# Three changes of order in a fused attention stage on one core: the residual addition ahead of the statistics, the input's transpose between two blocks of transposes, and a subtraction in halves

## The reference, cut to what matters

```python
x = x + L0_xattn(layernorm(x), ctx, ctx)      # 128 sequences of 64 rows, width 128, 16 heads of 8, causal
x = x + L0_ffn(layernorm(x))                  # 64 experts, top 8 of 64, plus one shared expert
x = x + L1_xattn(layernorm(x), ctx, ctx)      # correlation by FFT, top 6 delays
x = x + L1_ffn(layernorm(x))                  # quantised input, ternary weights

# L0_xattn: one matrix Wq projects q, k and v
qh, kh, vh = split(q @ Wq + bq), split(k @ Wq + bq), split(v @ Wq + bq)
weights = softmax(where(causal, qh @ kh.T / sqrt(8), -1e10))
return (weights @ vh) @ Wo + bo
```

## Time and profile before

| what | us |
|---|---|
| median of three runs (1264.62 to 1271.6) | 1265.1 |
| profiled execution, device time | 1266.42 |
| its span | 1264.6 |
| attention, about the first 304 us: loop steps 18 to 47 | 127.95 |
| PE busy, whole span | 1214.1 (96%) |
| DVE busy, whole span | 1061.9 (84%) |

### The profile page before, as it was taken

One profiled execution on the slowest core, in us unless ns is written; L12 is line 12 of the kernel. 1 busy time (PEld: TensorE's weight loads), 2 busy tenths in 40 slices (PEclk: granted clock), 3 DMA queues, 4 the chain that ended last, 5 costly groups with the idle time before them and its releaser, 6 DMA issues. The chain is left out here.

```text
span 1264.6 us, 28435 instructions
## 1 busy us (share of the span) xinstructions
PE 1214.1 (96%) x9881; PEld 997.0 (79%) x9881; DVE 1061.9 (84%) x2053; ACT 920.0 (73%) x1600; POOL 766.2 (61%) x829
## 2 busy tenths in 40 slices
PE   7899999998999999999999999999999999899976
PEld 5677777776888888888888888888888888799965
DVE  5989999895887978978978979879879887689986
ACT  4689898886777776777777777777777776777761
POOL 4766766662755755665656656656656633577773
PEclk9999999998999999999999999999999999999998
DMA  5511111104787677777677776776776786111004
GB/s 127 112 32 29 33 29 34 32 24 101 175 186 181 170 186 173 181 174 177 177 170 178 184 177 169 180 177 169 185 178 166 183 189 164 38 31 34 18 2 133
DMA packets 126174, 159.99 MB, mean 127 GB/s; under 512 B 20840, under 2 KB 59504, under 8 KB 126064
## 3 DMA queue, kind: packets, MB, share of 16 engines
q1 hardware_dynamic: 120750, 156.06, 51.2%
q10 hardware_dynamic: 5314, 2.53, 0.7%
HBM read 152.25 MB, written 6.29 MB: 125 GB/s over the span
## 5 line engine op out<-in xcount | busy, mean ns | idle before, releaser
L1147 ACT ACTIVATE e_pu<-e_pu 128x1024 f32<-128x1024 f32 x256 | 258.7, 1010 | 203.3 <-PE e_pu L1183 203.1
L1084 DVE TENSOR_TENSOR e_m<-e_pu,raw 128x1024 f32<-128x1024 f32 x256 | 310.0, 1211 | 94.0 <-ACT e_pu L1147 93.9
L1004 POOL TENSOR_TENSOR e_ml<-e_m,e_mh 128x1024 fp32r<-128x1024 f32 x80 | 192.5, 2407 | 145.9 <-ACT e_mh L1157 144.4
L1157 ACT CAST e_mh<-e_m 128x1024 fp32r<-128x1024 f32 x256 | 267.3, 1044 | 4.9 <-DVE e_m L1084 4.9
L1089 DVE TENSOR_TENSOR e_ml<-e_m,e_mh 128x1024 fp32r<-128x1024 f32 x176 | 241.0, 1369 | 25.7 <-ACT e_mh L1157 25.7
L1181 PE MATMUL e_pu<-r_xh,wuh 128*128 128x512 f32 x528 | 214.7, 407 | 0.7 <-PEq L211 0.7
L1183 PE MATMUL e_pu<-r_xl,wuh 128*128 128x512 f32 x528 | 209.3, 396 | 0.0
L1193 PE MATMUL e_py<-e_mh,wdl 128*128 128x512 f32 x528 | 209.2, 396 | 0.0
L1182 PE MATMUL e_pu<-r_xh,wul 128*128 128x512 f32 x528 | 209.2, 396 | 0.0
L1192 PE MATMUL e_py<-e_mh,wdh 128*128 128x512 f32 x528 | 208.1, 394 | 0.0
L1196 PE MATMUL e_py<-e_ml,wdh 128*128 128x512 f32 x528 | 167.3, 395 | 0.1
(11 more groups left out here) (225 smaller groups left out, 2351.1 us busy)
## 6 DMA issues: line engine op xcount, KB each, us to landing
raw<-gates_scratch SPq DMA_DIRECT2D x512, 256.0 KB, 4.3
x_res<-in_x_dram SPq DMA_DIRECT2D x64, 64.0 KB, 1.9
xcT<-in_ctxT_dram SPq DMA_DIRECT2D x64, 64.0 KB, 2.0
held<-in_ctx_dram SPq DMA_DIRECT2D x32, 128.0 KB, 2.1
raw<-in_L_ffn_W_up_dram SPq DMA_DIRECT2D x4, 512.0 KB, 4.7
raw<-in_L_ffn_W_down_dram SPq DMA_DIRECT2D x4, 512.0 KB, 5.6
gates_scratch<-raw SPq DMA_DIRECT2D x16, 128.0 KB, 2.3
out_dram<-t_res SPq DMA_DIRECT2D x8, 256.0 KB, 3.0
```

Source lines behind the costliest of these rows:

```text
L1004: nc.gpsimd.tensor_tensor(flat(ml[k][:]), flat(m[k][:]), flat(mh[k][:]).bitcast(F32), ALU.subtract).then_inc(m_low[1], 1)
L1084: nc.vector.tensor_tensor(flat(m[r % 3][:]), flat(pu[r % 3][:]), flat(gt[i % SPREAD]), ALU.mult).then_inc(gated, 1)
L1147: nc.scalar.activation(flat(pu[k][:]), flat(pu[k][:]), ACT.Silu).then_inc(silued, 1)
L1157: nc.scalar.copy(flat(mh[k][:]), flat(m[k][:])).then_inc(m_high, 1)
```

## The change

Three edits, all in `attention`. On DVE, `add_out` now stands ahead of `stats_of` and `aggregate`. On PE, two of the four transposes of `turn_probs` move behind `turn_in`; the semaphore `p_turned` rises after the fourth, as before. On POOL, `low_part` runs in each step of the loop on 264 columns, where it ran in each second step on 528.

```diff
-                order = ((invert_sum, 6), (scale_out, 6), (shift, 4), (norm, 1), (stats_of, 0), (aggregate, 0),
-                         (add_out, 6), (route, 0), (row_max, 3))
+                order = ((invert_sum, 6), (scale_out, 6), (shift, 4), (norm, 1), (add_out, 6), (stats_of, 0),
+                         (aggregate, 0), (route, 0), (row_max, 3))
...
-                    cols = bass.ds((t // 4 - peeled // 4) * piece, piece)
-                    wait_apart(pool, high, t + 2 * k + 2, idle["pool"])
-                    nc.gpsimd.tensor_tensor(cst[("wul", "wdl")[k]][:, cols], raw[:, k, cols],
-                                            cst[("wuh", "wdh")[k]][:, cols].bitcast(F32), ALU.subtract).then_inc(raw_read, 1)
+                    cols = bass.ds((t // 4 - peeled // 4) * piece + (k % 2) * (piece // 2), piece // 2)
+                    wait_apart(pool, high, t + k + 1, idle["pool"])
+                    nc.gpsimd.tensor_tensor(cst[("wul", "wdl")[k // 2]][:, cols], raw[:, k // 2, cols],
+                                            cst[("wuh", "wdh")[k // 2]][:, cols].bitcast(F32), ALU.subtract).then_inc(raw_read, 1)
...
-                    if not isinstance(t, int) and r % 2 == 1:
-                        low_part(t - r, r // 2)
+                    if not isinstance(t, int):
+                        low_part(t - r, r)
...
-                        act.wait_ge(raw_read, looped // 2 - peeled // 2)
+                        act.wait_ge(raw_read, looped - peeled)
...
                 def turn_probs(t, r):
                     at_least(pe, exped, t + 1)
                     at_least(pe, p_out, 2 * t - 1)
-                    for j in range(4):
+                    for j in range(2):
+                        nc.tensor.transpose(ppT[:, j, :], prob[:, r % 2, 2 * j:2 * j + 2].rearrange("p a k -> p (a k)"),
+                                            cst["ident"][:])
+
+                def turn_probs_on(t, r):
+                    for j in range(2, 4):
                         ins = nc.tensor.transpose(ppT[:, j, :], prob[:, r % 2, 2 * j:2 * j + 2].rearrange("p a k -> p (a k)"),
                                                   cst["ident"][:])
                     ins.then_inc(p_turned, 1)
-
-                def turn_probs_on(t, r):
                     at_least(pe, p_out, 2 * t)
```

## The result

| | before | changed |
|---|---|---|
| median of 20 runs, us | 1268.49 | 1272.13 |
| lowest to highest, us | 1264.62 to 1274.25 | 1267.02 to 1277.13 |
| profiled execution, us (its span) | 1266.42 (1264.6) | 1276.51 (1274.7) |

The ratio is 1.0033 with a 95% interval of 1.0018 to 1.0047: the changed kernel is a third of a per cent slower. I had predicted 1263.9 us within 1258 to 1270, that is, a small gain. I had predicted it from a median of three runs, 1265.1 us, and that was low: over 20 runs the kernel before has 1268.49. So 3.4 of the 8.2 us between forecast and result are the base that I started from, and the change itself is +3.6 us by the medians where I had -1.2. The two profiled executions lie further apart, 10.1 us, with a mean granted clock of 0.992 before and 0.983 after.

What follows compares the result with a forecast made beforehand. Circles of waits crossing engines were taken to bound the attention steps. Loop -2.1, steps 49 to 51 -0.7, steps 9 to 11 +0.6, steps 53 to 60 +1.0 sum to -1.2 us from 1265.1: 1263.9 us, range 1258 to 1270.

Steps and rivals of the forecast that it cites:

- steps 49 to 51: Where project waits 0.66 us for ACT's copies behind turn_in, the earlier turn_in gains 0.22 us a step, -0.7 us.
- the step that failed: Steps 9 to 11: POOL idles only before L409, and aggregate comes 0.2 us later behind add_out, +0.6 us.
- The term that I did have: Steps 53 to 60: row_max, behind a routing operation and the wait for out_project, comes 0.12 us later, +1.0 us.
- Rival B: DVE becomes the bound: add_out waits at the queue's head, row_max and aggregate late; 4.32 us a step, 1269.2 us, chance 0.22.
- The circle of two steps that I named: Loop: aggregate, POOL's work to kx, scores, weigh, out_project, back to aggregate; 8.22 us for two steps, 4.11 a step.
- a circle of its own, 4.08 us: Loop, through POOL and norm: norm ends with kx, so add_out starts at kx's end; 3.40 + 0.25 + 0.43 us.
- my sign of "in all four": Loop: norm lasts over 0.5 us in all four steps of a turn.
- 0.18 for other causes: Loop, per step: 0.06 us for scale_out waiting for its reciprocal at heads of turns, 0.03 for circles meeting in aggregate.
- a sign of being wrong: Loop: turn_in waiting for v_copy would show the forecast wrong; no size given for the sign.
- that circle: Loop: turn_in, six transposes, turn_o, o_copy, v_copy, back to turn_in; 4.05 to 4.14 us, said to bind nothing below 4.20.
- Two rules against the rows: Loop headroom by PE's busy share (5 us) or weight loads' share (30 us), and POOL-DVE contention speaking against the halves.

Runs made afterwards that it cites:

- the filled one: The changed kernel with 16 unread products on PE ahead of the wait for kx in steps 9 to 14, 53 and 54; 1.0147, 1289.1 us.

## Why the prediction was wrong, point by point

| us | forecast | measured |
|---|---|---|
| loop | -2.1 | -0.1 |
| steps 49 to 51 | -0.7 | -0.2 |
| steps 5 to 8 | none | -1.2 |
| steps 8 to 12 | +0.6 | +1.7 |
| steps 12 to 16 | none | +3.6 |
| step 52 to 53 | none | +1.25 |
| steps 53 to 61 | +1.0 | +2.3 |
| steps 16 to 18, 61 to 66 | none | -0.3, +0.5 |
| attention | -1.2 | +7.5 |
| behind it, at a lower clock | none | +2.6 |

The last column is the difference of the two profiles.

**The written-out steps: the step that failed.** I put steps 9 to 11 at +0.6 us by "`aggregate` comes later by the `add_out` ahead of it, 0.2", and said nothing of steps 12 to 16, nor of step 52. I counted the duration of `add_out` and forgot its wait. Where POOL has long work, PE is late because of POOL (`kx`), and before the change `aggregate` did not depend on PE at all, so that POOL could start its next step at once. Step 13 shows it. Before, on DVE and POOL:

```profile
64.36 0.18 DVE L263 BATCH_NORM_AGGREGATE a_mv<-a_stats 128x2 f32<-128x6 f32 x1
64.96 0.29 DVE L295 TENSOR_TENSOR x_res<-x_res,pob 128x128 f32<-128x128 f32 x1 [0.42 <-PE pob L618]
...
65.00 0.22 POOL L409 TENSOR_SCALAR a_ve<-a_mv 128x1 f32<-128x1 f32 x1
```

and after:

```profile
66.52 0.29 DVE L295 TENSOR_TENSOR x_res<-x_res,pob 128x128 f32<-128x128 f32 x1 [1.94 <-PE pob L621]
66.73 0.29 DVE L259 BATCH_NORM_STATS2 a_stats<-x_res 128x6 f32<-128x128 f32 x1
67.05 0.18 DVE L263 BATCH_NORM_AGGREGATE a_mv<-a_stats 128x2 f32<-128x6 f32 x1
...
67.32 0.22 POOL L409 TENSOR_SCALAR a_ve<-a_mv 128x1 f32<-128x1 f32 x1 [1.81 <-DVE a_mv L263]
```

`add_out` waited for `out_project` in both. Before, its wait stood behind the statistics and cost nobody; now it stands ahead of them, DVE sits 1.94 us, and POOL 1.81 us at the moment when it is the slowest engine. PE's late product and POOL's long work were side by side and are now one behind the other. The loss in steps 8 to 16 is 5.3 us where I had 0.6, and with the order taken back there nine tenths of it are gone. How much of it is the wait at a full clock, and how much PE's slower work at the lower level, is settled only for steps 8 to 12 (0.3 and 1.4); for steps 12 to 16, where no profile with the new order but the filled one kept the clock, it stays open. Part of the 1.94 us above is such slow work: from `row_max` to `row_max` this step had a clock of 0.53 (0.70 before), and two of PE's single transposes in it took 0.42 us each. It is also where the two causes meet. In the order before, that step took 5.78 us at 0.70 and, in the profile of the POOL edit alone, 5.78 at 1.00: a slow PE cost nothing, since nothing that POOL waits for hung on it. In the new order it took 7.01 us. Two runs with the new order (the pair without the PE edit, and the new order only outside the loop) met 0.70 in it and took 5.78 as well; they lost in the two steps behind it, 6.1 at 0.94 against 5.05 and 6.8 at 0.55 against 3.93.

Step 52 shows the wait at a clock of 1.00 in both kernels. There POOL's long work (2 us of routing) stands right behind L414, and PE is late by a product of the routing and by ACT's copies, not by `kx`. Before:

```profile
232.94 0.18 DVE L263 BATCH_NORM_AGGREGATE a_mv<-a_stats 128x2 f32<-128x6 f32 x1
234.22 0.29 DVE L295 TENSOR_TENSOR x_res<-x_res,pob 128x128 f32<-128x128 f32 x1 [1.10 <-PE pob L618]
...
233.21 0.22 POOL L409 TENSOR_SCALAR a_ve<-a_mv 128x1 f32<-128x1 f32 x1 [2.10 <-DVE a_mv L263]
...
236.50 1.03 POOL L386 TENSOR_TENSOR kx<-qkT,hmask 128x512 f32<-128x512 f32 x1
```

and after:

```profile
237.67 0.29 DVE L295 TENSOR_TENSOR x_res<-x_res,pob 128x128 f32<-128x128 f32 x1 [1.47 <-PE pob L621]
...
238.20 0.18 DVE L263 BATCH_NORM_AGGREGATE a_mv<-a_stats 128x2 f32<-128x6 f32 x1
...
238.47 0.22 POOL L409 TENSOR_SCALAR a_ve<-a_mv 128x1 f32<-128x1 f32 x1 [3.05 <-DVE a_mv L263]
...
241.78 1.03 POOL L386 TENSOR_TENSOR kx<-qkT,hmask 128x512 f32<-128x512 f32 x1
...
242.96 0.32 PE L560 MATMUL ps<-maskk,maskq 32*64 32x128 bf16 x16 [1.31 <-POOL kx L386]
```

`aggregate` stood 1.28 us ahead of `add_out` and now stands 0.53 us behind it; POOL starts late, and PE then waits 1.31 us for `kx`, for which it didn't wait before. From 52 to 53 that is 5.39 us against 4.14. In steps 52 to 55 the loss is 3.1 us: 1.4 to 1.5 by the new order at a clock of 1.00, most of it in this one step, and 1.6 by the clock (5.73 us at 0.70 from 53 to 54, against 4.06 to 4.14 at 1.00). The term that I did have, +1.0 for the eight steps from 53 on, was near where the clock held: 32.82 us with the DVE edit alone against 32.18, +0.6. Rival B had this mechanism in words, `add_out` waiting at the head of the queue and `aggregate`'s lateness reaching the scores over `kx`, but priced the written-out steps at +2.3; these three stretches lost 8.4.

**The clock: missing from the prediction.** The longer gaps of PE are often, not always, followed by single steps at the lower level. Of the runs, those with a mean granted clock of 0.988 or more were 23 of 29 of the kernel before in one set, at a mean of 1267.0 us, and 3 of 20 of the changed kernel, at 1269.1; below 0.986 it was 3 of 29 at 1273.1 and 14 of 20 at 1274.1. A second set of the kernel before had 17 of 35 runs at 0.988 or more, at 1267.6 us, and 15 below 0.986, at 1271.3. So at a like clock the changed kernel is 1 to 3 us slower, and the rest of its +3.6 us is that it is granted the low clock more often. The clocks of the 20 runs of the kernel before in the main comparison aren't on record, and the share of low runs went from 3 of 29 to 15 of 35 with no edit at all, so this split is rough. The halves alone met the low clock in 8 of 12 runs, with the written-out steps unchanged; why isn't shown, since the profiled one kept it.

**The loop: right circle, one term too small.** I forecast 4.20 us a step and got 4.263. The circle of two steps that I named is the one that sets it. Its terms, from the rows above: `aggregate` at 151.59 to the end of `kx` at 155.06 is 3.47 us (3.40 predicted); to L566 0.26 (0.26); to `weigh` 0.57 (0.54); `weigh` to the end of `out_project` 3.46 and 3.24 (3.31); from there to `aggregate` 155.69 - 154.74 = 0.95 (0.71). The last is the mis-sized one: over the four steps of a turn it is 0.88 to 0.98, 0.92 in the mean, and the excess of 0.21 us is two thirds of what the sum lacked. In every second step `add_out` doesn't start 0.03 us behind `out_project` but 0.2 to 0.3, since `norm` is held until `kx` is done, 154.42 + 0.72; I had summed that hold as a circle of its own, 4.08 us, and not as a term of the larger one. In the other two steps `norm` isn't held (0.34 us), against my sign of "in all four"; there `add_out` starts 0.14 to 0.17 us behind `out_project`, and `stats_of` 0.29 to 0.36 behind it where I took 0.25. Two steps take 2 x 4.263 = 8.53 us in the mean, against the 8.22 of my sum (to which I had added 0.18 for other causes). The POOL edit by itself gave 2.3 us, and the DVE edit took them back.

**Edit 1's gain came where nothing was queued behind it.** Steps 5 to 8 are 1.2 us faster: 4.03 to 4.08 us each, which were 4.20 to 4.75. I hadn't counted these steps. In the loop `weigh` no longer waits for `add_out`, as predicted, but PE spends what that freed on waiting for `kx` (6.0 us in 16 waits over the 30 steps).

**Edit 2.** No gain in the loop by itself, as forecast (128.00). Beside the DVE edit it shortens the way from `weigh` to the end of `out_project` from 3.39 to 3.32 us in the mean of a turn and gives 2.2 us over the loop; `project` starts 0.11 us behind `turn_o` in each step, where without the PE edit it started 0.16 to 0.23 us behind. I had called it nearly nothing. In steps 49 to 51 it gave 0.2 us, not 0.7: two or four products of the routing stand there ahead of `turn_in`, and they wait for `v_copy`. With the PE edit alone they start at 224.74, 0.14 us behind its end, and `turn_in` starts 1.71 us behind `weigh` (223.28 to 224.99) where it was 1.76 before (224.65 to 226.41), not 0.22 less. In the loop of the changed kernel, too, `turn_in` waits for `v_copy` in two steps of four, which I had called a sign of being wrong: `v_copy` ends at 152.65, `turn_in` starts at 152.80, 0.47 us behind the start of the two transposes where it is 0.27 without a wait. This took 0.05 to 0.2 us of such a step; the rest of that circle did not set it, since the scores stood behind `kx` there.

**Two rules against the rows.** By PE's busy share 5 us were to be had, by the weight loads' share 30. The Trainium skill's page "Perfetto Trace Analysis", section "Identifying the Most-Contended Engine", judges by the latter. No version took more than 2.7 us out of the loop, and the shortest loop, 125.27 us, has the weight loads at 79%: what holds is a chain across engines, which neither share shows. `norm` is held by POOL: it takes 0.72 us in the rows of the changed kernel and 1.23 in the loop of the DVE edit alone, where a whole low part is ahead of `kx`. The Trainium skill's page "GPSIMD Engine Reference", section "Specifications", names the contention between POOL and DVE, and for `norm` the trace agrees; it didn't speak against the halves, which gained 2.3 us.

## What to carry to other kernels

An operation that waits must be placed by what is queued behind it, not by how long it runs: in a step with slack it costs its duration, and in a step where the engine behind it is the slowest it costs up to the whole wait (in step 52 1.25 us, for an operation of 0.29 us that waited 1.47). An order that is the same for all steps of a pipeline should be tried by kinds of steps; here the same edit gained 1.2 us in three light steps and lost 5.3 in eight heavy ones; of what could be told apart there and in steps 52 to 55 (4.8 us), 3.0 came by way of the clock. When circles of waits across engines are summed, an interlock that holds an instruction belongs into each circle that passes through it.

## What the runs showed of the hardware

- DVE's `norm` (128x128, 0.34 us alone) ended with the POOL operation in flight: 0.56 us in the earlier trace rows, 0.72 in the changed kernel, 0.97 in steps 12 and 13 of the kernel before, each within 0.1 us of the end of that operation (`kx` in the first two, others in steps 12 and 13). `shift`, which reads PSUM, ran beside the same POOL operations in its usual 1.22 us.
- With gaps of PE of 0.8 to 2.2 us in the steps around it the granted clock over 50 to 90 us was 0.83; with the gaps filled it was 1.00. The same four waits of 0.54 to 1.67 us were followed by 0.70 in one profile and by 1.00 in another. At the lower level, 1.2 GHz, a transpose took 0.42 us instead of 0.27.
- 16 products of 64 columns in f32 stand in the trace as 32 matmuls and kept PE 3.8 us, 0.12 each, no less than a transpose of 128 columns (0.11 from start to start).
